# A third pair of PSUM banks for the backward row transform, and one down product placed between its groups

## The reference

```python
xn = _ln(xp, ln1w, ln1b)
xf = jnp.fft.rfft2(xn, axes=(1, 2), norm='ortho')
...   # two complex 64x64 products with relu, then a mask by THR
xs = jnp.fft.irfft2(xc, s=(H, W), axes=(1, 2), norm='ortho')
x = residual + jnp.transpose(xs, (0, 3, 1, 2))
xp2 = _ln(jnp.transpose(x, (0, 2, 3, 1)), ln2w, ln2b)
h = jax.nn.gelu(xp2 @ mw1 + mb1, approximate=False)
m = h @ mw2 + mb2
return x + jnp.transpose(m, (0, 3, 1, 2))
```

## Time and profile before

| what | value |
|---|---|
| median of 3 runs | 3486.16 us (3478.28 to 3488.5) |
| profiled execution | 3486.93 us, its span 3484.7 us |
| TensorE busy | 3155.1 us, 91% |
| VectorE busy | 2444.3 us, 70% |
| ScalarE busy | 2206.8 us, 63% |
| GpSimd busy | 1690.2 us, 49% |

### The profile page before, as it was taken

How to read it: one execution, slowest core, us unless ns; L and a number is a source line. 1 busy time by engine, 2 the same in 40 slices (tenths; PEclk the granted TensorE clock), 3 DMA queues, 4 the chain that set the end, 5 groups by cost and what they waited for, 6 DMA issues and landing times. The chain is left out here.

```text
span 3484.7 us, 65682 instructions
## 1 busy us (share of the span) xinstructions
PE 3155.1 (91%) x24429; PEld 1870.7 (54%) x24429; DVE 2444.3 (70%) x4302; ACT 2206.8 (63%) x3605; POOL 1690.2 (49%) x1421
## 2 busy tenths in 40 slices
PE   6945699999999999998989999999999999979689
PEld 2735364746474646464646464646565656344257
DVE  4956768677777777767677777677768676536667
ACT  3954466666666666767676666575757575636468
POOL 4435556464646465555464655545455643210242
PEclk7967899999999999999999999999999999989789
DMA  9860011120102021313120211111111111457898
GB/s 327 273 202 19 32 37 58 41 68 31 68 31 68 35 69 39 120 43 141 50 90 32 68 43 62 43 55 44 55 44 55 44 55 45 169 181 208 267 291 241
DMA packets 250332, 334.92 MB, mean 96 GB/s; under 512 B 22304, under 2 KB 195616, under 8 KB 242608
## 3 DMA queue, kind: packets, MB, share of 16 engines
q1 hardware_dynamic: 241664, 315.29, 26.9%
q0 software_dynamic: 7904, 15.57, 1.7%
q10 hardware_dynamic: 464, 0.02, 0.0%
HBM read 188.06 MB, written 142.74 MB: 95 GB/s over the span
## 5 line engine op out<-in xcount | busy, mean ns | idle before, releaser
L1612 ACT ACTIVATE images<-a_wide,a_up_b 128x1024 f32<-128x1024 f32 x512 | 569.7, 1113 | 251.8 <-PE a_wide L1806 248.6
L1806 PE MATMUL a_wide<-images 64*128 64x512 f32 x2048 | 579.4, 641 | 25.5 <-ACT images L1612 24.8
L1343 POOL TENSOR_TENSOR images<-a_o,a_mag 128x256 f32<-128x256 f32 (+1 forms) x512 | 360.3, 730 | 371.6 <-DVE a_mag L1451 368.7
L1301 POOL TENSOR_TENSOR images<-images,a_stat 128x512 f32<-128x512 f32 x256 | 267.5, 1046 | 544.7 <-DVEq L1502 528.2
L1817 PE MATMUL a_result<-images 128*64 128x512 f32 x2048 | 495.9, 605 | 1.8 <-DVE images L1466 1.8
L1431 DVE TENSOR_TENSOR a_o<-a_pair,a_mix_b 128x512 f32<-128x512 f32 (+1 forms) x272 | 181.0, 666 | 248.6 <-PE a_pair L1758 241.8
L1774 PEld LDWEIGHTS a_pair<-a_dft_h,a_g 128*128 128x128 f32 x2080 | 272.4, 191 | 129.0 <-issue 129.0
L1466 DVE TENSOR_TENSOR images<-a_result,images 128x512 f32<-128x512 f32 x256 | 176.0, 687 | 207.9 <-PE a_result L1832 207.6
L1806 PEld LDWEIGHTS a_wide<-images 64*128 64x128 f32 x2048 | 156.8, 185 | 287.6 <-issue 258.6
L1488 DVE TENSOR_REDUCE a_stat<-a_sq 128x16 f32<-128x1024 f32 x240 | 290.9, 1212 | 22.4 <-ACT a_sq L1646 20.8
L1817 PEld LDWEIGHTS a_result<-images 128*64 128x64 f32 x2048 | 124.4, 136 | 322.6 <-issue 319.0
(11 more groups left out here) (213 smaller groups left out, 6210.6 us busy)
## 6 DMA issues: line engine op xcount, KB each, us to landing
rows<-images SPq DMA_DIRECT2D x112, 512.0 KB, 2.9
images<-rows SPq DMA_DIRECT2D x105, 512.0 KB, 3.8
box_xc<-in_x SPq DMA_DIRECT2D x16, 1024.0 KB, 17.0
box_x<-in_x SPq DMA_DIRECT2D x64, 256.0 KB, 4.5
turned<-box_o SPq DMA_DIRECT2D x64, 256.0 KB, 3.7
images<-turned SPq DMA_DIRECT2D x16, 1024.0 KB, 11.9
planes<-box_work SPq DMA_DIRECT2D x64, 256.0 KB, 3.6
box_xc<-planes SPq DMA_DIRECT2D x16, 1024.0 KB, 20.2
```

The costliest lines, as they stand in the source:

```text
L1301: G.tensor_tensor(rows(y2[:, i % 2]), x[:, row:row + HB], r[:, :, None].broadcast_to([P, HB, C]), ALU.mult).then_inc(s_y2, 1)
L1343: ins = G.tensor_tensor(y[n % 2][:, :, to].rearrange("p c k -> p k c"), o2[:, j % 3, lo:4, r], mask[:, lo:4], ALU.mult)
L1612: A(hidden[:, i % 2, j], wide[:], ACT.Gelu, bias=up_b2[:, l, j:j + 1]).then_inc(s_hid, 1)
L1806: mm = M(wide[:, half * BANK:(half + 1) * BANK], up_fold[cs, l, j * P:(j + 1) * P], yc[cs, i % 2], start=True, stop=True)
```

## The change

Group i of `backward` now takes pair i % 3 of three, where the third is `wide` (groups 2 and 5), and waits for the additions of group i - 3. Three edits keep `wide` apart from the MLP: group 2 waits for the first gelu of step Q = 16 (n - 1) + 11, which reads `wide`; `mlp_up(Q, 1)` of that step waits also for the additions of group 5; and `mlp_down(Q - 1)` moves from behind group 7 to between groups 4 and 5. ScalarE's and VectorE's programs keep their order; only the banks that they read change. The last run's MLP, beside which no backward pass runs, is as before, and run 0's pass has no MLP beside it.

```diff
--- before.py
+++ after.py
@@ -1126,9 +1126,13 @@
 
             return bass.AP(iy.tensor, start * C + 8 * i, [[2 * KW * C, P], *([step * C, count] for step, count in steps), [1, 8]])
 
+        def pair_of(i):
+
+            return (pair[0], pair[1], wide)[i % 3]
+
         def of_kh(i):
 
-            return pair[i % 2][:].rearrange("p (k t h c) -> p k t h c", k=2, c=8, t=2)
+            return pair_of(i)[:].rearrange("p (k t h c) -> p k t h c", k=2, c=8, t=2)
 
         def mask_of(j):
 
@@ -1600,7 +1604,7 @@
                     act.wait_ge(s_ih, C // 8 * n + i + 1)
                     if i >= 2:
                         act.wait_ge(s_iy, C // 8 * n + i - 1)
-                    ends_of_kh = bass.AP(pair[i % 2], (quarter - 1) * 8, [[2 * BANK, P], [BANK + quarter * 8, 2], [1, 8]])
+                    ends_of_kh = bass.AP(pair_of(i), (quarter - 1) * 8, [[2 * BANK, P], [BANK + quarter * 8, 2], [1, 8]])
                     A(iy_rows(i, quarter, [HALF, 2]), ends_of_kh, ACT.Copy)
                     A(first_half_of(i), of_kh(i)[:, :, 1], ACT.Copy).then_inc(s_first_half, 1)
 
@@ -1785,14 +1789,18 @@
                     if i == 0:
                         pe.wait_ge(s_masked, N_CHUNK * (n + 1))
                         pe.wait_ge(s_ends, n + 1)
-                    if i >= 2:
-                        pe.wait_ge(s_iy, C // 8 * n + i - 1)
+                    if i == 2 and n:
+                        pe.wait_ge(s_hid, HC * (BLOCKS * (n - 1) + BACKWARD_SLOT // 4) + 1)
+                    if i == 5 and n:
+                        mlp_down(BLOCKS * (n - 1) + BACKWARD_SLOT // 4 - 1)
+                    if i >= 3:
+                        pe.wait_ge(s_iy, C // 8 * n + i - 2)
                     for c in range(8):
                         for part in range(2):
                             to = slice(part * HALF, (part + 1) * HALF)
                             for odd_kh in range(2):
                                 kh = slice(odd_kh * HALF, (odd_kh + 1) * HALF)
-                                mm = M(bank[2 * (i % 2) + odd_kh][to].rearrange("p (h c) -> p c h", c=8)[:, c], y[n % 2][kh, 8 * i + c, to],
+                                mm = M(pair_of(i)[to, odd_kh * BANK:(odd_kh + 1) * BANK].rearrange("p (h c) -> p c h", c=8)[:, c], y[n % 2][kh, 8 * i + c, to],
                                        dft_hi[kh, 0:HALF], start=True, stop=True)
                     mm.then_inc(s_ih, 1)
 
@@ -1801,6 +1809,8 @@
                     pe.wait_ge(s_yc, i + 1)
                     if i or j:
                         pe.wait_ge(s_hid, HC * i + j)
+                    if j and i % BLOCKS == BACKWARD_SLOT // 4 and i < BLOCKS * (RUNS - 1):
+                        pe.wait_ge(s_iy, C // 8 * (i // BLOCKS + 1) + 6)
                     for half in range(2):
                         cs = slice(half * C, (half + 1) * C)
                         mm = M(wide[:, half * BANK:(half + 1) * BANK], up_fold[cs, l, j * P:(j + 1) * P], yc[cs, i % 2],
@@ -1850,7 +1860,7 @@
                         parts(n, q, s, inverse, forward, spectrum, backward)
                         if s == (3 if q in CLOSED else 2 if q == 4 else 1) and 0 <= Q < BLOCKS * RUNS:
                             mlp_up(Q, 1)
-                        if s == (3 if q in CLOSED else 2) and 0 <= Q - 1 < BLOCKS * RUNS:
+                        if s == (3 if q in CLOSED else 2) and 0 <= Q - 1 < BLOCKS * RUNS and (q != BACKWARD_SLOT // 4 or n == RUNS - 1):
                             mlp_down(Q - 1)
                     if 0 <= Q + 1 < BLOCKS * RUNS:
                         mlp_up(Q + 1, 0)
```

## The result

The changed kernel is slower: a median of 3502.07 us (3493.49 to 3506.14, 6 runs) against 3484.92 us of the kernel before in the same comparison (3478.28 to 3490.09, 6 runs), a ratio of 1.0045 with a 95% interval of 1.0034 to 1.0056. The profiled execution took 3493.49 us, span 3491.2, 6.5 more than the span before. It is the shortest of its six.

A forecast was written before the change was run, and what follows sets the result against it. TensorE was taken as the bound, its bank waits in the backward passes lying over waits for instruction blocks. Savings of 4 + 1.6 + 2.2 + 1.4 = 9 us, 1 kept back, gave 3486.2 - 8 = 3478 us, range 3462 to 3491.

The forecast's parts named there:

- the pass at 710: Backward pass beginning at 710.00, worked out step by step: inverse transform at 727.66 instead of 727.81, 0.15 us saved.
- the third rival: TensorE's clock falls to half speed behind the merged pause in every pass: 13 us more, 3499 us; chance 0.10.
- What bounds the pass: Backward pass: TensorE stops for instruction blocks of some 128 matmuls, 4.00 and 3.73 us apart, against 2.1 us to run them.
- The first rival: Backward passes: instructions are no limit, 3.4 us saved in each of 13, 50 us in all, 3436 us; chance 0.07.
- some 45 us of issue gaps: Backward groups on TensorE: waits for VectorE all but vanish, while waits for instructions grow from 9.9 us to some 45.
- The wait for group 5's additions: New wait of the second up product of step 11 in a pass, 0.24 us after TensorE could start.
- 0.3 us in the mean of the 13: Saving in each of the 13 passes without staging copies, 4 us in sum.
- The sum of idle time around the pause hardly changes: TensorE in a pass: argument against added clock falls behind the merged pause, which were given a chance of 0.10.
- 1 us kept back for the clock: Taken off the summed saving of 9 us, for the merged pause and the clock, leaving 8 us.
- The staged passes and the first: Passes at 1560 and 1740, with a ScalarE staging copy, and the first, without MLP: 1.6, 2.2 and 1.4 us saved.
- only VectorE's chain is left: Staged pass at 1560: with three pairs only VectorE's additions set the inverse's start, at 1577.35 instead of 1578.92, saving 1.6 us.
- Theory 2: Explanation tested in the follow-up runs: moving the down product did the harm, by its lost cover over the gelu.

## Why the prediction was wrong

It gave 3478 us, a range of 3462 to 3491, and no measurable change as the likeliest; measured are 3502.07 us. Its reading of the bound held, and so did the steps of the pass at 710. It failed in the weight of the third rival, above all, and in one mean.

- **What bounds the pass** was right. The first rival, that instructions are no limit, fell: 57.3 us of "issue" stand where 61.4 us of bank waits were, and with half the calls a pass took the 14.4 us that it named, though with groups and waits of somewhat other lengths. The forecast of some 45 us of issue gaps was of the right size.
- **The pass at 710**: 17.66 forecast, 17.73 measured. The wait for group 5's additions was 0.46 us, not 0.24: the rest of group 4 took 717.90 - 717.40 = 0.50 us, not 0.34, so the additions came later. The gelu's wait was 1.30, forecast 1.28. From the third block's arrival to the inverse it took 726.74 - 717.40 = 9.34 us, where the forecast had 727.66 - 718.66 = 9.00. That the total still fits is luck: the block came 3.73 us behind the second, not 4.00.
- **"0.3 us in the mean of the 13"** is the first mis-sized term. It would have given 17.55; the six clean passes take 17.90, so 0.35 x 13 = 4.6 us are missing. They lie behind the third block, in those same 9.34 us: all six clean passes have them, also where TensorE stops for the fourth block and not for the additions, as at 878:

```profile
886.73 0.57 PE L1803 MATMUL a_pair<-a_dft_hi,images 64*64 64x64 f32 x21 [2.19 <-issue]
...
896.07 1.12 PE L1726 MATMUL a_pair<-a_g,a_idft_e 128*128 128x512 f32 x2
```

- **"The sum of idle time around the pause hardly changes", and 1 us kept back for the clock**: this is the step that failed. The rival's mechanism came true: the sum of idle time is no guard. It now stands in two pieces of 1.3 to 2.5 us some 4 us apart, the second in front of the moved down product. Six passes at 0.91 or 0.89 take 19.63 us instead of 17.90, and one at 0.97 takes 0.43 more: 6 x 1.73 + 0.43 = 10.8 us. The rival's price for a fall was 1.7 us, measured 1.73 (the six take 10.96 to 11.51 us behind the third block, the clean ones 9.34); its number of falls, 12 or 13, was too high and my 0.10 for it too low. I had taken "no fall in the pass at 710" for the rule, though three passes of before, one in five, had fallen under the same load.
- **The staged passes and the first** were forecast at 16.4, 17.0 and 16.95 us; they took 17.62, 17.02 and 16.33, 0.6 more in sum. In the first of these "only VectorE's chain is left" was wrong: 1.72, 1.65 and 0.39 us of "issue" and the gelu's wait of 1.31 set its length. The 1.2 us that it is over are half made up by the pass without an MLP, which was only taken by likeness.

The terms add up for the profiled execution: 4.6 + 10.8 + 0.6, less the 1 us kept back, is 15.0 us over its forecast of 3478.9, and it took 3493.5, 14.6 over. They don't reach the median. The 17.85 us from which the forecast took its 0.3 have two falls in them; without these they are 17.72. Both profiled executions of the changed kernel, 3493.5 and 3494.7, are at the short end of its runs. The mean granted clock of the six runs goes with their time, 0.959 and 0.958 for the two under 3496 us and 0.954 to 0.957 for the four over 3500, which points to more falls in these; no profile of such a run was had, so some 8 us of the median stay argued and not shown.

Theory 2 named a part of it. Behind the third block a clean pass takes 9.34 us with the down product moved and 9.13 without (the run with three pairs alone): 0.2 us, which I put down to the lost cover over the gelu. The fall costs 1.7 us instead of mostly 0.1, since the product stands just behind the pause, where a slow clock hurts most, instead of in it. The totals of clean passes, 17.90 and 17.38, differ by more, but the rest lies ahead of the third block and is not there in the second profile (17.55). Why one pause for a block is followed by a fall and the next is not stays open.

## What to carry to other kernels

Before a wait is taken away, look at what the engine would stand still for next in the same stretch: here the stops 128 matmuls apart said that TensorE's instructions came at their own pace, and many small matmuls were the bound under the bank's wait. Work moved into a pass belongs ahead of the point where the engine stands still, not behind it; one group earlier turned a loss of 0.45% into a gain of 0.4%, and the large products spread over the small ones, with the turns moved too, gave 1%. Long pauses close together can be worse than the same time in short ones: with two pairs and the down product moved, more idle time in pieces of 1.3 us brought no fall. It is no rule, since with half the calls falls followed waits of 0.58 and 1.30 us. A mechanism seen in three passes of 16 deserves its share of the chance.

## What the runs showed of the hardware

- TensorE's instructions come in packets of 16.4 KB, one for some 128 matmuls with their loads. Small matmuls of 64 x 64 x 64, at 2.1 us for 128, run through a packet's worth faster than the next one comes: in the changed kernel the stops ended 3.7 to 4.3 us apart in most passes (3.5 to 4.6 in all). The Trainium skill (Runtime: NRT & Kernel Launch, Instruction fetch mechanics) calls this cost mostly hidden; here it set the length of a pass, and the measurement decides.
- The clock's falls follow pauses or waits of TensorE, but not each of them. In the changed kernel's pass at 1911.90, whose clock stayed at 1.00, the pause was longer than the 1.94 us that a fall followed in the pass at 2081 (timeline of TensorE):

```profile
1920.39 0.58 PE L1803 MATMUL a_pair<-a_dft_hi,images 64*64 64x64 f32 x24 [2.20 <-issue]
```

- Which passes fell changed between two profiles of the same kernel. The Trainium skill (TensorE: Matmul & The Clock Gate, Part 1) says that the activity count runs free of the kernel's start, with which this agrees. A fall cost 0.1 us where TensorE would have waited in any case (three pairs alone, six passes) and 1.7 where it had work.
